# Starting the pass of a linear-attention transformer at another step, with the attention turned ahead of the projections and the query map ahead of the output projection

## The chip, the cores and the metric

The kernel runs on one core of one Trainium2 chip. The metric is the device time of one execution of the whole program in microseconds (us). The engines are named as the profile names them: PE is TensorE's matmuls and PEld its weight loads, DVE is VectorE, ACT is ScalarE, POOL is GpSimd, SP is SyncE, which issues the DMAs.

## What is computed

An input of 8 sequences of 512 tokens with 128 features goes through four stages, each of which adds its result to the input: an attention stage, a mixture of experts, a transformer of six layers with linear attention, and the mixture of experts again. The change touches the transformer stage alone. Cut to that stage:

```python
for l in range(6):                                    # out: 8 sequences x 512 tokens x 128
    q, k, v = out @ Wq[l] + bq[l], out @ Wk[l] + bk[l], out @ Wv[l] + bv[l]   # 16 heads of 8
    Qp, Kp = phi(q, omega[l]), phi(k, omega[l])       # exp(+-x omega - |x|^2 / 2): 16 features
    scores = tril(Qp @ Kp.T)                          # within a chunk of the sequence
    num = scores @ V + Qp @ kv_pre                    # kv_pre: sum over the earlier chunks
    den = scores.sum(-1) + Qp @ ks_pre
    a = (num / (den + eps)) @ Wo[l] + bo[l]
    h1 = layer_norm(out + a) * g1[l] + be1[l]
    y = relu(h1 @ W1[l] + bf1[l]) @ W2[l] + bf2[l]
    out = layer_norm(h1 + y) * g2[l] + be2[l]
```

## The kernel before, in words

`transformer_block` works on one sequence of 512 tokens (four tiles of 128) at a time, all in float32. The work on a sequence in one layer is cut into named steps. Two sequences are under way at once: a *slot* runs the first half of the steps (phase `in`, turn to S0) for one sequence between the steps of the second half (attend, output projection, feed-forward; phases `mix` and `out`) of the sequences before it. There are eight sequences, so eight slots a layer and 48 sequences' worth of work in six layers, with short runs `LEAD`, `FIRST`, `TAIL` and `END` at the two ends of the stage.

What each step is, on which engine:

- `turn`: ACT copies the tokens to `o_now` (L1168), PE transposes them into the PSUM bank w0 (L1022), ACT copies them to `oT` (L1171).
- `project`: PE multiplies by the query weights into w1 and by the key weights into w0 (L1032). ACT evacuates each bank in four activations, the value and the square of each of two halves (L1177, L1179): first `qq` from w1, then `kk` from w0.
- `values`: PE, four token tiles into w1 (L1037); DVE adds the bias into `v_tok` (L1272).
- `mapq`, `mapk`: PE multiplies `qq` into w0 and w1, `kk` into s0 and s1 (L1046); ACT takes the exponential (L1187).
- `keys`, `sums`: transposed keys (L1054, DVE copy L1290) and their sums with the values (L1065, DVE L1295, L1309, L1319).
- `S0`, `S1`: the scores of the two halves of the heads, 64 small matmuls each (L980); DVE masks them into `mixed` (L1328).
- `A0`, `A1`: attend, small matmuls on `mixed` and on the sums into n0 or n1 (L1000, L1004); ACT copies to `num` (L1191).
- `nums`: PE transposes `num` into w0 and n1 (L1089). DVE adds eps to the denominators, takes the reciprocal and multiplies, once for w0 and once for n1 (L1336, L1339, L1341), which makes `att` and frees the two banks.
- `att`: PE transposes `att` into n0 (L1096), ACT copies it to `attT` (L1194).
- `Wo`: PE multiplies `attT` by the output weights into w1 (L1105). DVE adds `o_bias` (L1349; POOL had made it of the tokens and the bias, L939), takes the statistics (L1247, L1251, L1253), waits for POOL's power (L943) and normalises (`Wo_norm`, L1260). POOL scales and shifts (L951, L954).
- `h1`: PE transposes the normalised tile into s2 (L1112), ACT scales it into `oT` (L1197).
- `F1`, `F2`: feed-forward (L1118, then ACT L1202 and DVE L1359; L1126, then DVE L1367, statistics and `F2_norm` as after Wo).
- `weights`: the copies of the next layer's weights for the `in` phase, once a layer. The copies for the `out` phase (`weights_out`: ACT L1155 and L1156, DVE L1237 to L1239, POOL L926 and L927) run once a layer ahead of the first slot, behind a wait for the steps before `slot.steps[0]`.

Each engine runs the steps of its slot in a fixed order: PE, ACT and POOL in the order of `SLOT`, DVE in that of `DVE`. The order within one engine is that of the program, and the engines meet at semaphores alone: `filled` and `emptied` of each PSUM bank, and one for each named event. `wait_free` waits until the bank's last fill has been evacuated, `ready` until the named step's fill has been. So a step placed too early makes everything behind it on its engine wait.

```python
SLOT = ("nums A0 S1 turn project att values Wo mapq A1 mapk h1 keys weights F1 sums S0 F2").split()
DVE = "nums S1 values Wo Wo_norm mapk keys weights F1 sums S0 F2 F2_norm".split()
```

In a layer the first four slots run in an inner loop of two rounds with two slots each, the other four are written out, and an outer loop goes over the first five layers. So each engine jumps back twice a layer, between the last step of one slot and the first of the next (a loop edge, below): F2 and nums on PE, F2 and A0 on ACT, F2_norm and nums on DVE.

Of the kernel before, what the change touches and what calls it, by code (L numbers as in the profile page):

```python
# [214 lines left out]
class AttentionPlan:  # L215
# [5 lines left out]
    LEAD = "X P0 P1 P2 L0 P3 L1 Xn St Yi Ys inc".split()  # L221
# [541 lines left out]
class TransformerPlan:  # L763


    SLOT = ("nums A0 S1 turn project att values Wo mapq A1 mapk h1 keys weights F1 sums S0 F2").split()
    LEAD = "turn project values mapq mapk keys sums S0".split()
    FIRST = "A0 S1 turn project values mapq A1 mapk keys weights sums S0".split()
    TAIL = "nums A0 S1 att Wo A1 h1 F1 F2".split()
    END = "nums att Wo h1 F1 F2".split()  # L770
    DVE = "nums S1 values Wo Wo_norm mapk keys weights F1 sums S0 F2 F2_norm".split()
    WITH = dict(Wo_norm="Wo", F2_norm="F2")
    FILLS = dict(weights="", turn="w0", project="w1 w0", values="w1", mapq="w0 w1", mapk="s0 s1", keys="w0 w1", sums="w0 w1",
                 S0="s0 s1 s2 s3", S1="s0 s1 s2 s3", A0="n0", A1="n1",
# [9 lines left out]
def transformer_block(nc, mem, ins, B):  # L784
# [17 lines left out]
    with ExitStack() as ctx:  # L802
# [3 lines left out]
        def sem(name):  # L806
# [52 lines left out]

        EVENTS = dict(o_now=1, o_bias=1, kz=4, kv_sum=3, v_tok=1, v_pad=1, den=2, inv=2,  # L860
                      stats=8, mv=8, eps=2, rstd=2, xn=8, scaled=2, h1b=1, o_new=1)
        PHASE = {n: "in" if n in ("o_now", "kz", "kv_sum", "v_tok", "v_pad") else "out" for n in EVENTS}
        s = {n: sem(n) for n in EVENTS}
        w_loaded = sem("w_loaded")
        made_in = {n: sem("made_in_" + n) for n in ("act", "dve")}
# [4 lines left out]
        with nc.Block() as block:  # L870
# [44 lines left out]
            @block.gpsimd  # L915
            def _(pool):
                pool.sem_inc(made_out["pool"], 1)

                def weights_in(l, slot):
                    pass  # L920

                def weights_out(l, slot):
                    wait_staged(pool, l, slot)
                    pool.wait_ge(s["o_new"], l * B + (B + 1))
                    pool.nop(nofuse=True)
                    nc.gpsimd.tensor_copy(rows[:].rearrange("p a n -> p (a n)"), next_rows[:, P:7 * P])  # L926
                    nc.gpsimd.tensor_tensor(be1_bf2[:], next_rows[:, 3 * P:4 * P], next_rows[:, 4 * P:5 * P],  # L927
                                            ALU.add).then_inc(made_out["pool"], 1)
                    pool.wait_ge(made_out["pool"], l + 2)
                    pool.nop(nofuse=True)  # L930

                def row(n):
                    return rows[:, n, :].unsqueeze(1).broadcast_to([P, TILES, P])

                def body(step, slot, sequence):
                    if step == "nums":

                        tokens = sequence_of(mem["o"], sequence["out"]).rearrange("p (c d) -> p c d", c=TILES)
                        nc.gpsimd.tensor_tensor(o_bias[:], tokens, row(0), ALU.add).then_inc(s["o_bias"], 1)  # L939
                    elif step in ("Wo", "F2"):  # L940
                        k = ("Wo", "F2").index(step)
                        wait(pool, "eps", slot, k + 1)
                        nc.gpsimd.tensor_tensor(m["rstd"][:], m["var_eps"][:],  # L943
                                                mem["minus_half"][:, 0:TILES], ALU.pow).then_inc(s["rstd"], 1)
                        wait(pool, "xn", slot, TILES * (k + 1))
                        pool.nop(nofuse=True)
                        g, b, out, name = (
                            (row(1), be1_bf2[:].unsqueeze(1).broadcast_to([P, TILES, P]), h1b[:], "h1b"),
                            (row(4), row(5), sequence_of(mem["o"], sequence["out"]).rearrange("p (c d) -> p c d", c=TILES),
                             "o_new"))[k]  # L950
                        nc.gpsimd.tensor_tensor(scaled[:], m["xn"][:], g, ALU.mult).then_inc(s["scaled"], 1)  # L951
                        wait(pool, "scaled", slot, k + 1)
                        pool.nop(nofuse=True)
                        nc.gpsimd.tensor_tensor(out, scaled[:], b, ALU.add).then_inc(s[name], 1)  # L954

                begin(pool, "o_bias rstd scaled h1b o_new")
                pipeline(pool, plan, weights_in, weights_out, body)

            @block.tensor
            def _(pe):  # L960
# [22 lines left out]
                            if u == SPANS - 1:  # L983
                                mm.then_inc(filled[f"s{r}"], 1)

                def attend(slot, t):

                    bank = f"n{t}"
                    if t == 0:
                        pe.wait_ge(s["v_pad"], slot.of("mix") + 2)  # L990
                        pe.wait_ge(s["kv_sum"], slot.of("mix") * 3 + 4)
                    wait_free(pe, bank, slot, f"A{t}")
                    for r in range(4):
                        wait_free(pe, f"s{r}", slot, f"A{t}")
                    pe.nop(nofuse=True)
                    for u in range(SPANS):
                        at = slice(u * SPAN, (u + 1) * SPAN)
                        if u:
                            for r in range(4):
                                nc.tensor.matmul(ps[bank][strip(r), at],  # L1000
                                                 kv[:, u - 1, 8 * t + 2 * r:8 * t + 2 * r + 2, :].rearrange("p h n -> p (h n)"),
                                                 phi_q[slot.parity][t][:, at], start=False, stop=False, skip_group_check=True)
                        for r in range(4):
                            mm = nc.tensor.matmul(ps[bank][strip(r), at],  # L1004
                                                  v_pad[:, u, 4 * t + r, :, :].rearrange("p h n -> p (h n)"),
                                                  mixed[t][r][:, u, :], start=u == 0, stop=u == SPANS - 1,
                                                  skip_group_check=True)
                    mm.then_inc(filled[bank], 1)

                def body(step, slot, sequence):  # L1010
# [64 lines left out]
                            ready(bank, "mapq")  # L1075
                        scores(slot, 0, slot.parity_in)
                    elif step == "S1":
                        pe.wait_ge(s["kz"], slot.of("mix") * 4 + 5)
                        scores(slot, 1, slot.parity)
                    elif step in ("A0", "A1"):  # L1080
                        attend(slot, int(step[1]))
                    elif step == "nums":

                        for t_ in range(2):
# [5 lines left out]
                            t.then_inc(filled[bank], 1)  # L1090
                    elif step == "att":
                        for bank in ("w0", "n1"):
                            ready(bank, "nums")
                        free("n0")
                        for c in range(TILES):
                            t = nc.tensor.transpose(ps["n0"][:, chunk(c)], att[:, c, :], mem["ident"][:])  # L1096
                        t.then_inc(filled["n0"], 1)
                    elif step == "Wo":
                        for made in (made_out["act"], made_out["dve"]):
                            pe.wait_ge(made, slot.layer + 2)  # L1100
                        pe.nop(nofuse=True)
                        ready("n0", "att")
                        free("w1")
                        for c in range(TILES):
                            t = nc.tensor.matmul(ps["w1"][:, chunk(c)], attT[:, chunk(c)], w_o[:],  # L1105
                                                 start=True, stop=True)
                        t.then_inc(filled["w1"], 1)
                    elif step == "h1":
                        wait(pe, "xn", slot, TILES)
                        free("s2")  # L1110
                        for c in range(TILES):
                            t = nc.tensor.transpose(ps["s2"][:, chunk(c)], m["xn"][:, c, :], mem["ident"][:])  # L1112
                        t.then_inc(filled["s2"], 1)
                    elif step == "F1":
                        ready("s2", "h1")
                        for f in range(FT):
                            free(f"s{f}")
                            nc.tensor.matmul(ps[f"s{f}"][:], w_1[:, chunk(f)], h1T[:], start=True,  # L1118
                                             stop=True).then_inc(filled[f"s{f}"], 1)
                    elif step == "F2":  # L1120
                        for f in range(FT):
                            ready(f"s{f}", "F1")
                        free("w1")
                        for c in range(TILES):
                            for f in range(FT):
                                t = nc.tensor.matmul(ps["w1"][:, chunk(c)], hid[f][:, chunk(c)], w_2[:, f, :],  # L1126
                                                     start=f == 0, stop=f == FT - 1)
                        t.then_inc(filled["w1"], 1)
# [698 lines left out]
```

## Time and profile before

| | |
|---|---|
| median of 3 runs | 4180.23 us (4180.0 to 4197.69) |
| the profiled execution | 4184.42 us, its span 4182.6 us |
| granted TensorE clock over the span | 0.939 of full |
| transformer stage | about 1800 us of the span, from some 2000 to some 3800 us |
| busy over the whole span | PE 87%, PEld 66%, DVE 62%, ACT 41%, POOL 22% |

A row of a timeline gives the start, the duration, the engine, the line, the operation and its tiles, merged over successive instructions of a kind (x4 is four of them); in square brackets is the engine's idle time before it and what ended that. A matmul here is of float32 and stands as two instructions in the trace, so a product of 128x512 is x2. The mean of one instruction is its duration and not its share of the stream, as matmuls overlap. A granted clock of 1.00 is TensorE's 2.4 GHz, 0.50 is 1.2 GHz.

### The profile page before, as it was taken

The page shows a single profiled execution, that of the slowest core. Times are in us where ns is not written, and L with a number is a line of the kernel's source. Part 1 is how long each engine was busy: PE and PEld are TensorE (multiplying, and loading weights), DVE is VectorE, ACT ScalarE, POOL GpSimd, SP SyncE. Part 2 cuts the span into 40 slices and gives each one's busy share as a digit, 9 for nine tenths or more (in the row PEclk, how much of TensorE's full clock was granted, in tenths as well). Part 3 has the DMA queues.
Part 4 walks back from the last instruction along what each step waited for, and adds up shares of the span by engine and source line. Part 5 has one row for each costly group of instructions (what it writes and reads, how often), then busy time and mean ns, then how long its engine had stood idle before and what let it go on. Part 6 is the DMA issues. An engine that isn't in the chain of part 4 may idle for free. (4 is left out here: it accounts for less than half of the span.)

```text
span 4182.6 us, 105516 instructions
## 1 busy us (share of the span) xinstructions
PE 3633.0 (87%) x39640; PEld 2780.1 (66%) x39640; DVE 2605.9 (62%) x6838; ACT 1712.6 (41%) x3438; POOL 901.5 (22%) x781
## 2 busy tenths in 40 slices
PE   4999999999999998996788888888888888886998
PEld 3767677777677776885566566666566666664887
DVE  4555555556555556887466666666666666665887
ACT  2555555555555553332333333333333333332332
POOL 3222232322223230000112222222222222221000
PEclk9999999999999999998888999999999889987999
DMA  2000000000000000000000000000000000000000
GB/s 86 24 28 21 28 23 25 26 25 24 27 25 23 24 23 4 1 1 13 14 2 2 15 2 2 15 2 2 15 2 3 15 2 2 2 2 0 1 0 21
DMA packets 38339, 59.63 MB, mean 14 GB/s; under 512 B 6960, under 2 KB 16688, under 8 KB 37552
## 3 DMA queue, kind: packets, MB, share of 16 engines
q1 hardware_dynamic: 37936, 53.78, 3.8%
q8 instruction: 312, 5.11, 0.5%
q14 instruction: 91, 0.75, 0.1%
HBM read 18.10 MB, written 2.10 MB: 5 GB/s over the span
## 5 line engine op out<-in xcount | busy, mean ns | idle before, releaser
L662 ACT ACTIVATE a_prob<-a_s,a_shift,a_scale 128x128 f32<-128x128 f32 (+3 forms) x512 | 312.0, 613 | 486.2 <-DVE a_shift L745 486.1
L943 POOL TENSOR_TENSOR t_rstd<-t_var_eps,minus_half 128x4 f32<-128x4 f32 x96 | 97.6, 1017 | 1219.3 <-DVE t_var_eps L1253 1219.3
L1539 ACT ACTIVATE ffn_silu<-ffn_ps_g 128x512 f32<-128x512 f32 x272 | 161.3, 599 | 382.7 <-PE ffn_ps_g L1489 370.6
L1482 PEld LDWEIGHTS ffn_ps_y<-moe_down,ffn_hidden 128*128 128x128 f32 x2176 | 282.1, 191 | 41.4 <-issue 19.9
L1482 PE MATMUL ffn_ps_y<-moe_down,ffn_hidden 128*128 128x128 f32 x2176 | 288.1, 275 | 17.4 <-DVE ffn_acc L1643 17.4
L1191 ACT COPY t_num<-t_n 128x512 f32<-128x512 f32 x96 | 56.3, 586 | 570.9 <-PE t_n L1004 570.9
L1643 DVE SCALAR_TENSOR_TENSOR ffn_acc<-ffn_ps_y,ffn_combine,ffn_acc 128x128 f32<-128x128 f32 x960 | 269.8, 345 | 8.9 <-DVE ffn_acc L1643 1.8
L1328 DVE TENSOR_TENSOR t_mixed<-t_s,upto 128x512 f32<-128x512 f32 x384 | 238.4, 683 | 21.6 <-PE t_s L980 20.2
L1655 DVE TENSOR_TENSOR ffn_hidden<-ffn_silu,ffn_ps_u 128x512 f32<-128x512 f32 x272 | 185.5, 684 | 106.2 <-ACT ffn_silu L1539 74.6
L742 DVE TENSOR_REDUCE a_neg_max<-a_s 128x2 f32<-128x256 f32 (+3 forms) x256 | 208.8, 816 | 68.1 <-PE a_s L565 65.6
L413 POOL TENSOR_TENSOR a_k_sin<-a_k_swap,sin_swap 128x512 f32<-128x512 f32 x64 | 81.5, 1274 | 733.3 <-DMA a_k_swap<-a_k_own 733.3
L594 PE MATMUL a_z<-a_probT,a_tok 128*64 128x128 f32 x2560 | 179.3, 278 | 40.8 <-ACT a_probT L651 40.8
L696 DVE TENSOR_TENSOR a_lin<-a_a,lin_mask 128x512 f32<-128x512 f32 x256 | 165.0, 687 | 79.0 <-PE a_a L489 79.0
L1004 PE MATMUL t_n<-t_mixed,t_v_pad 128*32 128x64 f32 x6144 | 197.1, 228 | 16.2 <-issue 8.5
L581 PE MATMUL a_t<-ident,a_prob 128*128 128x128 f32 x1280 | 203.2, 283 | 8.1 <-ACT a_prob L662 4.2
L561 PE MATMUL a_s<-a_keys,a_query 64*128 64x128 f32 (+3 forms) x1024 | 203.7, 471 | 1.1 <-issue 0.5
L1004 PEld LDWEIGHTS t_n<-t_mixed,t_v_pad 128*32 128x32 f32 x6144 | 150.6, 115 | 80.1 <-issue 80.0
L980 PE MATMUL t_s<-t_phi_q,t_kz 32*128 32x64 f32 x6144 | 197.2, 274 | 6.0 <-issue 5.4
L980 PEld LDWEIGHTS t_s<-t_phi_q,t_kz 32*128 32x128 f32 x6144 | 184.2, 187 | 16.9 <-issue 8.2
L581 PEld LDWEIGHTS a_t<-ident,a_prob 128*128 128x128 f32 x1280 | 150.3, 144 | 66.8 <-issue 50.6
L651 ACT COPY a_probT<-a_t 128x512 f32<-128x512 f32 (+2 forms) x384 | 188.1, 528 | 5.8 <-PE a_t L581 3.9
L1126 PE MATMUL t_w<-t_w,t_hid 128*128 128x128 f32 x1536 | 184.2, 278 | 2.3 <-DVE t_hid L1359 2.3
(209 smaller groups left out, 8878.8 us busy)
## 6 DMA issues: line engine op xcount, KB each, us to landing
a_k_swap<-a_k_own SPq DMA_DIRECT2D x128, 128.0 KB, 2.1
a_y_swap<-a_y_own SPq DMA_DIRECT2D x128, 128.0 KB, 2.0
a_staged<-in_pairs SPq DMA_DIRECT2D x8, 384.0 KB, 4.0
t_next<-in_t_w SPq DMA_DIRECT2D x12, 256.0 KB, 3.1
t_next_rows<-in_t_rows SPq DMA_DIRECT2D x6, 448.0 KB, 4.1
x<-in_x SPq DMA_DIRECT2D x8, 256.0 KB, 5.3
out<-x SPq DMA_DIRECT2D x1, 2048.0 KB, 8.7
t_next_sq<-in_t_sq SPq DMA_DIRECT2D x6, 256.0 KB, 2.7
```

What stands on the lines that cost most here:

```text
L561: nc.tensor.matmul(ps[f"s{h}"][:, 0:(c + 1) * P], query[slot.parity][rows(h), own], keys[slot.parity][rows(h), 0:(c + 1) * P], start=True, ...
L581: t = nc.tensor.transpose(ps[bank][:, (at + j) * P:(at + j + 1) * P], prob[c % 2][h][:, j * P:(j + 1) * P], mem["ident"][:])
L651: nc.scalar.copy(probT[c % 2][:, hs, 0:n], ps[bank][:, 0:2 * n // len(banks)].rearrange("p (h n) -> p h n", n=n)).then_inc(emptied[bank], 1)
L662: nc.scalar.activation(prob[c % 2][h][:, 0:(c + 1) * P], ps[f"s{h}"][:, 0:(c + 1) * P], ACT.Exp, bias=shift[:, k:k + 1], scale=scale[slot. ...
L742: nc.vector.tensor_reduce(neg_max[:, two], ps_s[:, :, 0:(c + 1) * P], AX.X, ALU.max, negate=True).then_inc(s["negs"], 1)
L980: mm = nc.tensor.matmul(ps[f"s{r}"][:, u * SPAN:(u + 1) * SPAN], kz[t][strip(r), u, :, :].rearrange("p h n -> p (h n)"), phi_q[parity][t][ ...
L1004: mm = nc.tensor.matmul(ps[bank][strip(r), at], v_pad[:, u, 4 * t + r, :, :].rearrange("p h n -> p (h n)"), mixed[t][r][:, u, :], start=u ...
L1126: t = nc.tensor.matmul(ps["w1"][:, chunk(c)], hid[f][:, chunk(c)], w_2[:, f, :], start=f == 0, stop=f == FT - 1)
L1328: nc.vector.tensor_tensor(mixed[t_][r][:], ps[f"s{r}"][:].rearrange("p (u n) -> p u n", u=SPANS), mem["upto"][:].unsqueeze(1).broadcast_to ...
L1482: t = nc.tensor.matmul(ps_y[e % 2][:, c * P:(c + 1) * P], hidden[e % 3][:, c * P:(c + 1) * P], w_down[:, e * P:(e + 1) * P], start=True, s ...
L1643: t = nc.vector.scalar_tensor_tensor(acc[:, c, :], y, combine[parity][:, c, e:e + 1], acc[:, c, :], ALU.mult, ALU.add)
L1655: nc.vector.tensor_tensor(hidden[e % 3][:], silu[e % 2][:], ps_u[e % 2][:], ALU.mult).then_inc(hid_done, 1)
```

## The change

The slot begins at `turn` instead of at `nums`, so that `nums A0 S1` stand at its end. Read as a ring, PE's and ACT's order differs from before in two places: `att` now comes right behind `turn`, ahead of `project`, and `mapq` comes ahead of `Wo`. DVE's `nums` comes ahead of `F2_norm`, where it came behind it. POOL's `o_bias` moves from `nums` to the start of `Wo`, which is the next thing that POOL does after F2's `o_new`, as before. `LEAD` takes over `A0 S1` and `FIRST` takes `nums A0 S1` at its end. What is waited for stays the same, with the counts fitted to the new place of the steps. The loop edges now lie between `S1` and `turn` on PE, between `A0` and `turn` on ACT and between `S1` and `values` on DVE; the copies of `weights_out` lie there too. No operation is added or taken away.

```diff
@@ class TransformerPlan
-    SLOT = ("nums A0 S1 turn project att values Wo mapq A1 mapk h1 keys weights F1 sums S0 F2").split()
-    LEAD = "turn project values mapq mapk keys sums S0".split()
-    FIRST = "A0 S1 turn project values mapq A1 mapk keys weights sums S0".split()
-    TAIL = "nums A0 S1 att Wo A1 h1 F1 F2".split()
-    END = "nums att Wo h1 F1 F2".split()
-    DVE = "nums S1 values Wo Wo_norm mapk keys weights F1 sums S0 F2 F2_norm".split()
+    SLOT = ("turn att project values mapq Wo A1 mapk h1 keys weights F1 sums S0 F2 nums A0 S1").split()
+    LEAD = "turn project values mapq mapk keys sums S0 A0 S1".split()
+    FIRST = "turn project values mapq A1 mapk keys weights sums S0 nums A0 S1".split()
+    TAIL = "att Wo A1 h1 F1 F2 nums".split()
+    END = "att Wo h1 F1 F2".split()
+    DVE = "values Wo Wo_norm mapk keys weights F1 sums S0 F2 nums F2_norm S1".split()
@@ events
-        PHASE = {n: "in" if n in ("o_now", "kz", "kv_sum", "v_tok", "v_pad") else "out" for n in EVENTS}
+        PHASE = {n: "in" if n in ("o_now", "kz", "kv_sum", "v_tok", "v_pad") else "mix" if n in ("den", "inv") else "out"
+                 for n in EVENTS}
@@ gpsimd body
-                    if step == "nums":
+                    if step == "Wo":
                         tokens = sequence_of(mem["o"], sequence["out"]).rearrange("p (c d) -> p c d", c=TILES)
                         nc.gpsimd.tensor_tensor(o_bias[:], tokens, row(0), ALU.add).then_inc(s["o_bias"], 1)
-                    elif step in ("Wo", "F2"):
+                    if step in ("Wo", "F2"):
@@ tensor
-                def attend(slot, t):
+                def attend(slot, t, parity):
...
-                        pe.wait_ge(s["v_pad"], slot.of("mix") + 2)
-                        pe.wait_ge(s["kv_sum"], slot.of("mix") * 3 + 4)
+                        wait(pe, "v_pad", slot, 1)
+                        wait(pe, "kv_sum", slot, 3)
...
                     elif step == "S1":
-                        pe.wait_ge(s["kz"], slot.of("mix") * 4 + 5)
-                        scores(slot, 1, slot.parity)
-                    elif step in ("A0", "A1"):
-                        attend(slot, int(step[1]))
+                        wait(pe, "kz", slot, 4)
+                        scores(slot, 1, slot.parity_in)
+                    elif step == "A0":
+                        attend(slot, 0, slot.parity_in)
+                    elif step == "A1":
+                        attend(slot, 1, slot.parity)
...
                     elif step == "att":
                         for bank in ("w0", "n1"):
-                            ready(bank, "nums")
+                            wait_free(pe, bank, slot, slot.steps[0])
```

## Rows read from the trace of the kernel before

**Rows 1.** The profile's page, its span and its first section (busy time)

```profile
span 4182.6 us, 105516 instructions
PE 3633.0 (87%) x39640; PEld 2780.1 (66%) x39640; DVE 2605.9 (62%) x6838; ACT 1712.6 (41%) x3438; POOL 901.5 (22%) x781
```

**Rows 2.** Stretches of one slot: busy us (instructions) of each engine; granted clock, DMA

```profile
2532.00:2545.00 13.00, 10.18 (x60) 5.68 (x62) 6.34 (x18) 7.53 (x12) 2.71 (x3) 0.74 0.01 1
2549.00:2562.00 13.00, 12.92 (x131) 9.98 (x130) 10.15 (x21) 4.36 (x9) 1.16 (x1) 1.00 0.01 3
```

**Rows 3.** PE's waits in the stage: total us, times, longest

```profile
PE t_w L1105 <- ACT t_attT L1194: 106.0, 48, 2.3
PE t_w L1022 <- DVE t_att L1341: 36.4, 39, 2.0
PE t_w L1032 <- ACT t_oT L1171: 35.1, 47, 0.8
```

**Rows 4.** PE's timeline, a slot of common length: start, duration, instructions, idle before

```profile
2528.91 2.01 PE L980 MATMUL t_s<-t_phi_q,t_kz 32*128 32x64 f32 x64
...
2531.79 0.66 PE L1022 MATMUL t_w<-ident,t_o_now 128*128 128x128 f32 x4 [0.87 <-DVE t_att L1341]
2533.19 3.78 PE L1032 MATMUL t_w<-t_oT,t_w_in 128*128 128x512 f32 x4 [0.75 <-ACT t_oT L1171]
...
2541.61 1.15 PE L1105 MATMUL t_w<-t_w_o,t_attT 128*128 128x128 f32 x8 [1.77 <-ACT t_attT L1194]
...
2547.94 1.98 PE L1046 MATMUL t_s<-t_kk,t_omega 128*128 128x512 f32 x4
2549.76 0.60 PE L1112 MATMUL t_s<-ident,t_xn 128*128 128x128 f32 x4
```

**Rows 5.** ACT's timeline of the same slot

```profile
2535.30 0.68 ACT L1177 ACTIVATE t_qq<-t_w,t_cols_in 64x512 f32<-64x512 f32 x1 [2.24 <-PE t_w L1032]
...
2540.89 0.59 ACT L1194 COPY t_attT<-t_n 128x512 f32<-128x512 f32 x1
...
2549.10 0.60 ACT L1187 ACTIVATE t_phi_k<-t_s 128x512 f32<-128x512 f32 x1 [0.46 <-PE t_s L1046]
2549.96 0.60 ACT L1187 ACTIVATE t_phi_k<-t_s 128x512 f32<-128x512 f32 x1 [0.26 <-PE t_s L1046]
```

**Rows 6.** DVE's timeline of the same slot

```profile
2528.36 0.17 DVE L1253 TENSOR_SCALAR t_var_eps<-t_mean_var 128x4 f32<-128x4 f32 x1
...
2532.25 0.42 DVE L1341 TENSOR_TENSOR t_att<-t_n,t_inv 128x256 f32<-128x256 f32 x1
...
2546.22 1.12 DVE L1260 TENSOR_SCALAR t_xn<-t_o_bias,t_mean_var,t_rstd 128x128 f32<-128x128 f32 x4 [1.13 <-POOL t_rstd L943]
```

**Rows 7.** PE's timeline of the shortest slot, from one S1 to the next

```profile
2756.96 2.01 PE L980 MATMUL t_s<-t_phi_q,t_kz 32*128 32x64 f32 x64
...
2776.22 0.60 PE L1112 MATMUL t_s<-ident,t_xn 128*128 128x128 f32 x4
...
2791.86 2.01 PE L980 MATMUL t_s<-t_phi_q,t_kz 32*128 32x64 f32 x64
```

**Rows 8.** Groups of PE's instructions in the stage: busy us, mean ns of one

```profile
L1126 PE MATMUL t_w<-t_w,t_hid 128*128 128x128 f32 x1504 | 180.4, 278 | 1.0 <-DVE t_hid L1359 1.0
...
L1046 PE MATMUL t_w<-t_qq,t_omega 128*128 128x512 f32 x184 | 137.9, 890 | 0.0
...
L1046 PE MATMUL t_s<-t_kk,t_omega 128*128 128x512 f32 x184 | 91.3, 618 | 0.0
L1105 PE MATMUL t_w<-t_w_o,t_attT 128*128 128x128 f32 x376 | 82.6, 388 | 105.4 <-ACT t_attT L1194 105.4
```

**Rows 9.** The copy of w_2, once a layer: ns min/median/max, first and last start

```profile
L1239 DVE COPY t_w<-t_next x6: 425/1040/1040, 2045.5 to 3534.7; 128x512 f32<-128x512 f32 x6
```

**Rows 10.** PE's and DVE's timelines at one loop edge

```profile
2638.64 0.65 PE L1089 MATMUL t_w<-ident,t_num 128*128 128x128 f32 x4 [2.01 <-issue]
...
2643.48 0.59 DVE L1237 COPY t_cols_v<-t_next_cols 128x6 f32<-128x6 f32 x1 [2.28 <-issue]
```

More of the change, by code:

```diff
@@ L1001, in attend @@
                                                  kv[:, u - 1, 8 * t + 2 * r:8 * t + 2 * r + 2, :].rearrange("p h n -> p (h n)"),
-                                                 phi_q[slot.parity][t][:, at], start=False, stop=False, skip_group_check=True)
+                                                 phi_q[parity][t][:, at], start=False, stop=False, skip_group_check=True)
                         for r in range(4):
```

## The prediction

> **What bounds the kernel now.** I read the page first: PE is busy for 87% of the span and no other engine for more than 62% [rows 1]. That alone would say that reordering can't bring much. The stretches of one slot say otherwise. Over 13 us in the feed-forward half PE is busy for 12.92 us at a granted clock of 1.00; over the 13 us behind S1 it is busy for 10.18 us at a clock of 0.74 [rows 2]. A mean of 0.74 between 1.00 and 0.50 is 52% of the stretch at 1.2 GHz, and a matmul at that level takes longer and so looks busy. So one half of a slot is bound by PE's work, and this change leaves it alone; the other, from the end of S1 to the start of h1, is bound by a chain of waits, and there the steps are moved.
>
> PE's waits name the links: 106.0 us for `attT` ahead of Wo, 36.4 us for DVE's `att` ahead of turn, 35.1 us for `oT` ahead of project [rows 3], 177.5 us or 3.7 us a slot. The timelines say why each is there. DVE makes `att` only after it has normalised F2's result, so w0 is freed late and turn starts 0.87 us after S1's end at 2530.92. Project waits 0.75 us for ACT's copy of `oT`. ACT then evacuates qq and kk in one go from 2535.30 to `attT` at 2540.89, and only behind these comes the copy for which Wo waits [rows 4, 5]. The stretch takes 2549.76 - 2530.92 = 18.84 us in this slot and 2776.22 - 2758.97 = 17.25 us in the shortest [rows 4, 7]. From S1 to S1 the shortest slot takes 34.90 us; the slot of common length takes 1.59 us more, 36.49, all of it in this stretch.
>
> **The new stretch, link by link.** I count from the end of S1 (zero), at full clock, with durations of the common slot.
>
> *Turn.* DVE's `nums` now follows the variance (ends 2528.53) without the wait for POOL and the normalisation. Now the second `att` ends at 2532.67, 1.88 us behind the normalisation's end at 2530.79 (`att` is six operations directly behind it). In the new order it ends at 2528.53 + 1.9, about 2530.4, and the first, which frees w0, 0.95 us earlier [rows 4, 6]. Both lie before S1's end, so turn starts at zero and `att` on PE finds its input ready. What pays is `F2_norm`: 1.9 us of nums less the 1.1 us for which DVE waited for POOL anyway [rows 6], so 0.8 us later, on a tile that isn't read for several slots. S1's masks end no later than before. Nothing on PE waits for either. Gain 0.87 us.
>
> *Project and att.* Project now starts 1.40 us after turn starts [rows 4], so at 1.40 still; but four transposes of `att` (0.6 us) fill PE's wait for `oT`, and ACT copies `attT` at 1.3 to 1.9, when it waited before. So att costs nothing at either place, and its copy of 0.6 us leaves the queue behind kk. In the new stretch PE has had 0.1 us of idleness before project instead of 1.62, so I take project at full clock: its first bank reaches ACT 1.16 us after its start, as `phi_k` (2549.10) follows mapk (2547.94) [rows 4, 5], where in the common slot it took 2.11 (2535.30 - 2533.19). ACT starts qq at 2.56 and is through with kk 5.59 us later [rows 5], at 8.15.
>
> *Mapq* needs w0, which kk frees, so it starts at 8.2; values, at 5.4, fits into the wait as now. That mapq waited behind Wo before and stands ahead of it now is no gain of its own: both need the end of kk. *Wo* needs w1 again, which the second exponential frees: mapk to the end of the second `phi_k` takes 2550.56 - 2547.94 = 2.62 us [rows 4, 5], so Wo starts at 10.8 + 0.1 = 10.9. This is a new wait, of some 0.8 us, and behind it on PE stand A1, mapk and h1.
>
> *h1.* From Wo's start to the end of the normalisation are 2547.34 - 2541.61 = 5.73 us [rows 4, 6], so h1 can start at 16.7. PE itself arrives there at 10.9 + 1.0 + 1.9 (A1) + 1.85 (mapk) = 15.65: what was late by PE's own work is now late by DVE's chain, and 1.0 us of PE's time is idle but covers a slow clock in A1 and mapk. Sum: 16.7 us where the shortest slot has 17.25, so a slot of 34.90 - 0.55 = 34.35 us. DVE's products behind h1 keep their distance to it.
>
> **The clock** is the unknown. Before, TensorE fell to 1.2 GHz in the stretches after turn's and project's waits and again around Wo and mapq. Mapq's matmuls take 890 ns on average where mapk's of the same shape take 618, so 4 x 0.272 = 1.09 us a slot; Wo's take 388 where F2's take 278, 8 x 0.110 = 0.88 us [rows 8]; together 1.97 us. In the new order mapq and Wo are both on the path. The bounds are nothing (full clock) and all of it: at 1.2 GHz mapq and Wo need twice their 1.95 and 1.15 us, 3.1 us more. PE idles there from 3.4 to 8.2 apart from values and again before Wo, so the clock will still fall in some slots. But one idle stretch stands where three stood, so I take less than half of the old loss, 0.85 us. A slot: 35.2 us.
>
> On this the Trainium skill speaks against the change. Its page "TensorE: Matmul & The Clock Gate", section "HAM oscillation — how this bites in real kernels", says that a waiting stretch between bursts of matmuls sends the clock back to half, every time round. The trace agrees that it falls (0.74, rows 2); if it did so in every slot for all of mapq and Wo, the loss would be the upper bound, the third rival.
>
> **The loop edges.** A layer takes (3534.7 - 2045.5) / 5 = 297.84 us [rows 9]; 8 x 36.49 are 291.9, so its two edges cost 5.9 us. At an edge PE stands 2.01 us for nothing that the profile shows, DVE 2.28 us, and at the layer's edge DVE's copies follow before it makes `att` [rows 10]. In the new order DVE's gap and copies fall between S1's masks (end 3.3) and values (its input at 6.6): 3.3 + 2.3 + 1.9 = 7.5, then v_tok until 8.8, which frees w1 in time for mapq's second bank at 9.1. PE's gap stays exposed, now ahead of turn, and the clock behind it will be low for project. 5.5 us a layer.
>
> The page "Runtime: NRT & Kernel Launch", section "Instruction fetch mechanics", says that a taken branch whose target isn't at hand stalls the fetch; that fits the 2.01 us and says that they stay wherever the edge is put.
>
> **Sum.** A layer: 8 x 35.2 + 5.5 = 287.1 us, 10.7 less. The 46 full slots are 5.75 layers' worth: 61.6 us. The short runs at the ends have the same steps; I count them at nothing. Against the profiled execution's 4184.4 us: 4122.8. The median of the runs is 4.2 us lower than it, so 4118.6; I say 4118.
>
> **Rivals.**
> 1. *The clock stays up.* A loss of 0.1 us: 8 x 34.45 + 5.5 = 281.1, 16.7 us less a layer, 96 in all, 4084. For it: att fills the first gap, and a shorter ring changes when the clock falls. Against: 4.8 us with only values in them.
> 2. *The clock falls as before.* The old loss of 1.97 us on mapq and Wo: 8 x 36.3 + 5.5 = 295.9, 11 us less in all, 4169. The freed waits come back as slow matmuls, and the measurement can't tell it from no change.
> 3. *Slower.* Mapq and Wo were in part beside each other's waits; now Wo, and DVE's chain behind it, come last in line behind mapq and ACT's exponential. With both at 1.2 GHz in every slot the loss is 3.1 us: 8 x 37.45 + 5.5 = 305.1, 42 us more, 4222. It decides from a loss of (297.84 - 5.5) / 8 - 34.35 = 2.2 us a slot.
> 4. *ACT's loop edge is uncovered.* ACT's edge lay in its long wait before A0's copy. Now it lies between A0's copy and `o_now`, for which turn waits, and at a layer's edge the copies of `w_o` wait there for S1. A gap like PE's runs beside PE's own and starts earlier, so at least nothing is lost; if ACT ends 1.5 us later than PE at each of 12 edges it is 18 us: 4136.
>
> **Chances and range.** The forecast, with its own range 4100 to 4150, 55%; rival 1, 13%; rival 2, 12%; rival 3, 10%; rival 4, 10%. Leaving rival 3 out, the range is 4084 to 4172. The kernel's measurement can tell about 0.5% (21 us) from no change: faster 0.78, within it 0.12, slower 0.10.
>
> **What would show it.** Right: PE's wait of turn for DVE gone, ACT's `attT` next to `oT`, mapq waiting for `kk`, Wo for `phi_q`, and h1 now waiting for `t_xn` by about 1 us; the distance between copies of w_2 at 287 us a layer. Wrong: mapq's mean near 890 ns or above and Wo's near 430 (rival 2 or 3); a wait of turn for ACT's `o_now` (rival 4); a wait of sums for `k_tok`, which would mean that DVE's masks of the keys, now beside POOL's scaling, have become slower.

## The result and the profile after

The changed kernel takes 4209.9 us (median; 4207.8 to 4214.7) against 4183.3 us before: the ratio is 1.0059, with a 95% interval of 1.0032 to 1.0085. By the ratio it is slower by 25 us, where I had forecast 62 us less (4118 against 4180). The time lies between the rivals 2 (4169) and 3 (4222), nearer to the third.

The page of the changed kernel, to be held against [rows 1], with the granted clock in slices:

```profile
span 4212.9 us, 105523 instructions
PE 3660.5 (87%) x39640; PEld 2803.4 (67%) x39640; DVE 2642.2 (63%) x6838; ACT 1708.6 (41%) x3438; POOL 913.9 (22%) x781
PEclk9999999999999998997899889888888888887999
```

The clock's slices before:

```profile
PEclk9999999999999999998888999999999889987999
```

The same 39640 matmuls keep PE busy for 27.5 us longer. In the transformer stage, from the 20th slice on, most of the clock's slices now read 8, where more than half read 9 before.

PE's timeline of one slot of common length in the changed kernel, from S1 to h1, as [rows 4]:

```profile
2504.73 2.01 PE L981 MATMUL t_s<-t_phi_q,t_kz 32*128 32x64 f32 x64
2506.67 0.66 PE L1023 MATMUL t_w<-ident,t_o_now 128*128 128x128 f32 x4
2507.16 0.60 PE L1099 MATMUL t_n<-ident,t_att 128*128 128x128 f32 x4
2508.08 1.98 PE L1033 MATMUL t_w<-t_oT,t_w_in 128*128 128x512 f32 x4 [0.32 <-ACT t_oT L1174]
2512.06 1.16 PE L1038 MATMUL t_w<-t_w_in,t_oT 128*128 128x128 f32 x8 [2.00 <-ACT t_qq L1182]
2514.85 3.78 PE L1047 MATMUL t_w<-t_qq,t_omega 128*128 128x512 f32 x4 [1.63 <-ACT t_kk L1182]
2519.32 2.07 PE L1108 MATMUL t_w<-t_w_o,t_attT 128*128 128x128 f32 x8 [0.69 <-ACT t_phi_q L1190]
...
2524.48 1.98 PE L1047 MATMUL t_s<-t_kk,t_omega 128*128 128x512 f32 x4
2526.30 0.60 PE L1115 MATMUL t_s<-ident,t_xn 128*128 128x128 f32 x4
```

S1 ends at 2506.74. Counted from there project starts at 1.34 (walk: 1.40), values at 5.32 (5.4) and mapq at 8.11 (8.2): up to here every link came as worked out. Then mapq takes 3.78 us and Wo 2.07, and A1, between Wo and mapk, 3.1 us where I had 1.9. h1 starts at 19.56 instead of 16.7.

The busy times of the engines and the granted clock in this slot, with the columns of [rows 2]: from the end of S1 to the start of h1, then in project, mapq, Wo, most of A1, and mapk:

```profile
2506.80:2526.40 19.60, 14.97 (x157) 9.30 (x158) 7.53 (x23) 8.90 (x14) 5.11 (x5) 0.74 0.01 2
2508.08:2510.06 1.98, 1.98 (x4) 0.67 (x4) 1.61 (x3) 1.17 (x3) 1.76 (x2) 1.00 0.00 0
2514.85:2518.63 3.78, 3.78 (x4) 1.17 (x4) 0.00 (x0) 0.60 (x1) 0.00 (x0) 0.50 0.02 4
2519.32:2521.39 2.07, 2.07 (x12) 1.85 (x16) 0.00 (x0) 0.00 (x0) 0.00 (x0) 0.50 0.00 0
2521.39:2524.10 2.71, 2.71 (x105) 2.71 (x109) 2.12 (x10) 0.00 (x0) 0.31 (x1) 0.50 0.02 6
2524.48:2526.30 1.82, 1.82 (x13) 0.81 (x6) 1.15 (x5) 1.18 (x2) 0.52 (x2) 1.00 0.00 0
```

So project and mapk have the full clock, and mapq, Wo and A1 between them 1.2 GHz throughout. In 41 of the 45 full slots that the trace shows whole, mapq takes 3.4 to 3.8 us; in the other four it takes 1.98.

PE's waits in the stage, against [rows 3], and the groups of mapq and Wo, against [rows 8]:

```profile
PE t_w L1038 <- ACT t_qq L1182: 91.6, 48, 2.0
PE t_w L1047 <- ACT t_kk L1182: 71.5, 48, 1.7
PE t_w L1023 <- issue: 33.3, 10, 3.7
PE t_w L1108 <- ACT t_phi_q L1190: 31.8, 46, 0.8
PE t_s L1115 <- DVE t_xn L1263: 19.8, 13, 6.2
PE t_w L1033 <- ACT t_oT L1174: 11.9, 39, 0.7
```

```profile
L1047 PE MATMUL t_w<-t_qq,t_omega 128*128 128x512 f32 x184 | 164.7, 1047 | 68.8 <-ACT t_kk L1182 68.8
...
L1108 PE MATMUL t_w<-t_w_o,t_attT 128*128 128x128 f32 x376 | 81.0, 382 | 32.5 <-ACT t_phi_q L1190 31.8 <-ACT t_attT L1197 0.7
```

The wait for `att` (36.4 us) is gone, of that for `attT` (106.0 us) 1.4 us are left, and that for `oT` fell from 35.1 to 11.9 us. But the wait of values for `qq` grew (from 40.1 us), those of mapq for `kk` (2.6 us before) and of Wo for `phi_q` are new, and mapq's matmuls went from 890 to 1047 ns. The copy of w_2 gives the length of a layer, as [rows 9]:

```profile
L1242 DVE COPY t_w<-t_next x6: 415/676/1039, 2058.7 to 3561.6; 128x512 f32<-128x512 f32 x6
```

(3561.6 - 2058.7) / 5 = 300.6 us against 297.8.

### The profile page after: what moved, and what is told of

Same layout as the page of the kernel before. It is cut to its first block and busy times, and to the rows that moved or that the text cites. A ratio compares the mean times of both kernels' runs of the same rounds, so it can differ in the third digit from the quotient of the medians.

```text
span 4212.9 us, 105523 instructions
## 1 busy us (share of the span) xinstructions
PE 3660.5 (87%) x39640; PEld 2803.4 (67%) x39640; DVE 2642.2 (63%) x6838; ACT 1708.6 (41%) x3438; POOL 913.9 (22%) x781
## 5 line engine op out<-in xcount | busy, mean ns | idle before, releaser
L1047 PE MATMUL t_w<-t_qq,t_omega 128*128 128x512 f32 x192 | 172.0, 1048 | 71.5 <-ACT t_kk L1182 71.5
L1005 PE MATMUL t_n<-t_mixed,t_v_pad 128*32 128x64 f32 x6144 | 219.1, 244 | 7.2 <-DVE t_mixed L1331 7.1
L1352 DVE TENSOR_TENSOR t_o_bias<-t_w,t_o_bias 128x512 f32<-128x512 f32 x48 | 33.2, 692 | 292.3 <-PE t_w L1108 286.2
L1275 DVE TENSOR_TENSOR t_v_tok<-t_w,t_bv 128x512 f32<-128x512 f32 x96 | 61.5, 682 | 224.1 <-PE t_w L1038 224.1
L1001 PE MATMUL t_n<-t_phi_q,t_kv 128*32 128x64 f32 x5376 | 193.2, 244 | 9.1 <-issue 9.1
```

The lines of the kernel that those rows point to most:

```text
L1001: nc.tensor.matmul(ps[bank][strip(r), at], kv[:, u - 1, 8 * t + 2 * r:8 * t + 2 * r + 2, :].rearrange("p h n -> p (h n)"), phi_q[parity][t ...
L1005: mm = nc.tensor.matmul(ps[bank][strip(r), at], v_pad[:, u, 4 * t + r, :, :].rearrange("p h n -> p (h n)"), mixed[t][r][:, u, :], start=u ...
```

## The experiments

Each was run beside the kernel before, whose median was 4181 to 4187 us from set to set; the ratios are against those runs. Differences between two variants are of their medians, so those between sets are good to some 6 us. Means per slot are of the 45 full slots that a trace shows whole; a slot is "at an edge" when a standstill at a jump back falls into it (12 of the 45, in the old order 13), and "away from the edges" otherwise.

My theory after the result, called *clock* below: PE is idle from project to `kk`'s end but for values, so the clock is at 1.2 GHz when mapq, Wo and A1 come. The rivals: Wo stands behind mapq and its exponential, and DVE's chain with it (*order*); the loop edges cost more at their new place (*edge*).

**1. Which of the moved steps does it?** Three variants of the changed kernel, which differ in the places of att and Wo alone.

e1_rotate:

```diff
-    SLOT = ("turn att project values mapq Wo A1 mapk h1 keys weights F1 sums S0 F2 nums A0 S1").split()
+    SLOT = ("turn project att values Wo mapq A1 mapk h1 keys weights F1 sums S0 F2 nums A0 S1").split()
```

> The changed kernel with att back behind project and Wo back ahead of mapq: what is left of the change is the start of the slot at turn (the loop edges and the copies of the out-phase weights lie there) and DVE's nums ahead of F2_norm. If the loss comes from the new order of att, mapq and Wo (clock or chain), this kernel keeps the 0.87 us a slot ahead of turn and lands at 4145 to 4175. If it comes from the place of the loop edges, it is at or above 4195.

Measured: 4137.5 us, ratio to before 0.9892 (0.9868 to 0.9915). The start at turn and the earlier `nums` alone are worth 47 us, somewhat more than expected. The edges at their new place are not the fault.

e2_att_early:

```diff
+    SLOT = ("turn att project values Wo mapq A1 mapk h1 keys weights F1 sums S0 F2 nums A0 S1").split()
```

> The changed kernel with Wo ahead of mapq again and att still ahead of project. By the theory that Wo's place behind mapq and its exponential is the fault (Wo at 10.9 us behind S1, then DVE's chain), Wo can now start when v_tok frees w1, at about 8.0, and h1 at about 15: 4115 or less. By the theory that the clock is the fault (PE idle from project to kk's end but for values, then everything at 1.2 GHz), Wo, mapq and A1 are still slow, 3 to 4 us on a path of 15: 4165 to 4190.

Measured: 4090.1 us, 0.9779 (0.9755 to 0.9804). That is the order theory's number, 120 us below the changed kernel, for the exchange of two steps. But the exchange touches the clock as well: mapq's mean is 820 ns where the changed kernel has 1047 (Wo's is 391 against 382), so the 120 us are not the order's alone. Part 3 holds the clock up in both orders.

e3_mapq_first:

```diff
+    SLOT = ("turn project att values mapq Wo A1 mapk h1 keys weights F1 sums S0 F2 nums A0 S1").split()
```

> The changed kernel with att back behind project, mapq still ahead of Wo. Wo's place decides: 4205 to 4215 as the changed kernel. If att's place decides (its four transposes fill PE's idle stretch behind project and keep the clock up), 4170 or less, and mapq's mean duration falls well under 1048 ns.

Measured: 4152.2 us, 0.9929 (0.9906 to 0.9952); the changed kernel is 58 us slower. With mapq first Wo waits for `phi_q` and not for `attT`, so att's place should be of no weight to the chain. Its groups of mapq and Wo:

```profile
L1047 PE MATMUL t_w<-t_qq,t_omega 128*128 128x512 f32 x184 | 117.3, 771 | 74.3 <-ACT t_kk L1182 74.3
L1108 PE MATMUL t_w<-t_w_o,t_attT 128*128 128x128 f32 x368 | 61.5, 318 | 31.8 <-ACT t_phi_q L1190 31.8
```

771 ns instead of 1047, with much the same waits ahead (74.3 and 31.8 us). Four transposes, 0.6 us of work, behind project instead of ahead of it made the difference. That speaks for the clock. ACT's order changed along with PE's, but in the common slots of both kernels mapq starts 8.11 us behind S1, so ACT's new order moved nothing ahead of it. The next runs leave ACT's order alone.

**2. Is it the clock?** Matmuls are repeated in the idle stretches. They write the same results again, so no wait becomes shorter; PE has only more to do.

e4_filler (the key projection three times, the values twice):

```diff
                         for bank, n in (("w1", 0), ("w0", 1)):
                             free(bank)
-                            nc.tensor.matmul(ps[bank][:], w_in[:, n, :], oT[:], start=True,
-                                             stop=True).then_inc(filled[bank], 1)
+                            for again in range(3 if n else 1):
+                                t = nc.tensor.matmul(ps[bank][:], w_in[:, n, :], oT[:], start=True, stop=True)
+                            t.then_inc(filled[bank], 1)
                     elif step == "values":
                         free("w1")
-                        for c in range(TILES):
+                        for c in list(range(TILES)) * 2:
```

> The changed kernel with matmuls repeated in the two idle stretches: the key projection three times instead of once, the values twice (same results, written again). Nothing waits for less. If the clock is the fault, mapq and Wo run at 2.4 GHz, mapq's mean falls from 1048 ns towards 620, and the time to 4090 to 4140 in spite of some 2.7 us more work a slot. If the chain through w1 and DVE is the fault, it stays at 4210 or gets slower.

Measured: 4145.4 us, 0.9910 (0.9885 to 0.9934), 64 us faster than the changed kernel with more to do, though 5 us short of the range that I expected. Its timeline of PE in one slot, and the clock from the end of S1 (2460.06) to h1:

```profile
2461.40 3.69 PE L1034 MATMUL t_w<-t_oT,t_w_in 128*128 128x512 f32 x8 [0.32 <-ACT t_oT L1175]
2465.38 2.05 PE L1039 MATMUL t_w<-t_w_in,t_oT 128*128 128x128 f32 x16 [0.28 <-ACT t_qq L1183]
2468.17 1.98 PE L1048 MATMUL t_w<-t_qq,t_omega 128*128 128x512 f32 x4 [0.74 <-ACT t_kk L1183]
2470.84 1.16 PE L1109 MATMUL t_w<-t_w_o,t_attT 128*128 128x128 f32 x8 [0.69 <-ACT t_phi_q L1191]
...
2476.62 0.66 PE L1116 MATMUL t_s<-ident,t_xn 128*128 128x128 f32 x4 [0.90 <-DVE t_xn L1264]
```

```profile
2460.10:2476.60 16.50, 13.60 (x168) 8.08 (x168) 7.00 (x21) 9.51 (x15) 4.47 (x4) 1.00 0.01 2
```

This is the walk of the prediction at full clock: mapq at 8.11 (walk 8.2), Wo at 10.78 (10.9), h1 at 16.56 (16.7), and PE waits 0.90 us for `t_xn` (1.0). Between this slot and that of the changed kernel lie 3.0 us, and the only difference ahead of mapq is PE's work.

Three microseconds in each of 46 slots would be 138 us and not 64. Two things take the rest. The mean from S1 to h1 falls by 1.97 us only (20.03 to 18.06), since the slots at an edge gain nothing: from S1 to S1 they take 39.68 us in the changed kernel and 40.19 here, the others 36.89 and 34.95. And S1 itself grows from 2.03 to 2.70 us on average, for waits that no semaphore explains (18.4 us in 31 times where the changed kernel has 0.6 us in 2). What is left is 1.30 us a slot, 60 us.

e8_key_twice and e11_values_twice (the changed kernel with one of the two repeats, the key projection twice or the values twice):

> The changed kernel with the key projection twice, 0.86 us of matmuls more in the idle stretch behind project and nothing else. att's four transposes moved back there (0.6 us) had brought 58 us. If that came of PE's work in this stretch keeping the clock up, and not of att's own place, this lands at 4135 to 4165. If it came of ACT's or DVE's order, it stays at 4205 to 4215.

> The changed kernel with values twice (1.0 us of matmuls more, between values and mapq), the key projection once. If any work between project and mapq keeps the clock up, as the key projection twice did (4131), it lands at 4130 to 4160. If it is the stretch between project and values that counts, it stays at 4190 to 4215.

Measured: 4131.3 us, 0.9873 (0.9846 to 0.9899), and 4143.8 us, 0.9898 (0.9877 to 0.9920). Mapq's mean is 721 and 668 ns. The first is 4 us below its expected range, the second within. With ACT's and DVE's order untouched, 0.86 us of matmuls more a slot took 79 us off, in whichever of the two stretches it is 66 us at least. So it is PE's idleness that costs, by way of the clock, and work in either stretch will do.

e5_before_filler (the kernel before, with the repeats of e4):

> The kernel before with the same repeated matmuls (key projection three times, values twice). By the walk at full clock its h1 starts 16.5 us behind S1 (turn at 0.9, project 2.3, kk's end 9.0, attT 9.6, Wo 9.75, mapq 10.7, A1 12.6, h1 16.4) where it has 18.4 now: 1.9 us a slot, 87 us, so about 4095. Then the cold clock was half of what bound the kernel before too. If the clock matters only in the changed order, it stays at 4175 to 4190.

Measured: 4160.6 us, 0.9937 (0.9914 to 0.9961). The direction is the clock theory's; the size is a quarter of the 87 us that I expected. Mapq and Wo are at full clock there (619 and 287 ns), and the stretch that I had walked came out as said: from S1 to h1 it takes 16.63 us on average instead of 18.51, 1.88 us less where I had 1.9. It is the other half of the slot that took back 0.82 us, and 0.64 of these are S1, which grew from 2.18 to 2.82 us. PE's waits in S1, first before and then in e5:

```profile
PE t_s L980 <- issue: 5.4, 9, 0.8
```

```profile
PE t_s L980 <- issue: 20.2, 37, 1.3
```

PE stands still in the midst of S1 for nothing that the profile shows. That leaves 1.06 us a slot or 49 us, and the profiled execution is in fact 43 us faster than the one before. The median of the seven executions lies 19 us above it (they go from 4141 to 4169 us), and why they differ so I can't tell.

**3. What is the order worth when the clock is up?** e6_att_proj2 is e2 with the key projection three times, e12_key_thrice the changed kernel with the same; they differ in whether Wo or mapq comes first.

> att early, Wo ahead of mapq (4090) with the key projection three times. If the clock falls for the idle stretch behind project, this takes most of the cold matmuls away: h1 at 15 to 15.5 instead of 16.9, 4010 to 4040. If only the stretch between values and Wo matters, it stays within 10 us of 4090.

> The changed kernel with the key projection three times: it differs from the version at 4043 in nothing but mapq standing ahead of Wo. By the walk at full clock h1 is at 16.7 us with mapq first and at 14.8 with Wo first: 1.9 us a slot, 85 us, so 4120 to 4135. If the order of the two is of no weight once the clock is up, it is 4043 too.

Measured: e6 4043.0 us, 0.9667 (0.9643 to 0.9691); e12 4136.3 us, 0.9881 (0.9857 to 0.9904). The order is worth 93 us, 2.0 us in each of 46 slots, where the walk says 1.9. Both are 1 to 3 us above the ranges that I expected. The timeline of e6, where S1 ends at 2460.30:

```profile
2461.73 3.69 PE L1034 MATMUL t_w<-t_oT,t_w_in 128*128 128x512 f32 x8 [0.32 <-ACT t_oT L1175]
2465.70 1.16 PE L1039 MATMUL t_w<-t_w_in,t_oT 128*128 128x128 f32 x8 [0.28 <-ACT t_qq L1183]
2468.24 1.16 PE L1109 MATMUL t_w<-t_w_o,t_attT 128*128 128x128 f32 x8 [1.37 <-DVE t_v_tok L1276]
2469.23 2.07 PE L1048 MATMUL t_w<-t_qq,t_omega 128*128 128x512 f32 x4
2473.05 1.98 PE L1048 MATMUL t_s<-t_kk,t_omega 128*128 128x512 f32 x4
2474.87 0.60 PE L1116 MATMUL t_s<-ident,t_xn 128*128 128x128 f32 x4
```

Since `attT` is ready at 2, Wo waits only for w1, which `v_tok` frees, and runs at 7.9 in the time for which mapq has to wait for `kk` anyway. DVE's chain starts 2.8 us earlier, `phi_q` is no longer ahead of it, and PE arrives at h1 without a stop.

e7_att_both (e6 and two more products of 128x512 into the free bank s3 ahead of Wo):

> As the one before, with two more products of 128x512 into the free bank s3 between values and Wo, so that PE has no long idle stretch left. Full clock nearly throughout, h1 at 14.8: 3995 to 4015. If these matmuls delay Wo instead, it is slower than the one before.

Measured: 4046.4 us, 0.9667 (0.9648 to 0.9687), as e6. That is 31 us above the range that I expected. Mapq's mean fell from 656 to 619 ns, and away from the edges the stretch from S1 to h1 became 0.3 us shorter (14.86 to 14.56), but S1 itself grew by as much (2.36 to 2.64), so from S1 to S1 nothing is gained (32.81 and 32.83).

**4. The other terms.** e10_nums_late is e6 with DVE's nums behind F2_norm again:

```diff
-    DVE = "values Wo Wo_norm mapk keys weights F1 sums S0 F2 nums F2_norm S1".split()
+    DVE = "values Wo Wo_norm mapk keys weights F1 sums S0 F2 F2_norm nums S1".split()
```

> The same version (4043) with DVE's nums behind F2_norm again, as before the change. By the walk the first att frees w0 0.9 us behind S1 and the second is done at 1.8, for which PE's att, now ahead of project, waits: project at 2.45 instead of 1.35, 1.1 us a slot, 50 us: 4085 to 4100. If DVE's order is of no weight, 4043.

Measured: 4088.7 us, 0.9769 (0.9751 to 0.9787), 46 us above e6. DVE's order was worth what the walk says. PE's waits for it come back:

```profile
PE t_w L1023 <- DVE t_att L1345: 18.6, 32, 1.1
...
PE t_n L1100 <- DVE t_att L1345: 8.1, 28, 0.3
```

e9_unrolled4 is e6 with `UNROLLED = 4`:

> The version with att early, Wo ahead of mapq and the key projection three times (4043), with the first four slots of a layer written out as one round of the inner loop instead of two rounds of two. The slot at each jump back is 37 to 38 us there against 32 to 33.7 for the others. If the jump itself is what costs, 4.5 us a layer go: 4010 to 4022. If it is the place in the layer or the entry and exit of the loop, nothing changes.

Measured: 4014.7 us, 0.9599 (0.9577 to 0.9621), 28 us below e6 and the fastest version of all. PE's wait ahead of turn, first of e6 and then of e9:

```profile
PE t_w L1023 <- issue: 36.6, 12, 3.8
```

```profile
PE t_w L1023 <- issue: 16.0, 4, 4.2
```

20.6 us of PE's standstill at turn are gone with the jump in the middle of the layer. The layer is (3390.7 - 2054.7) / 5 = 267.2 us long by the copy of w_2, against (3410.5 - 2053.0) / 5 = 271.5 in e6.

## Why the prediction was wrong

**What bounds the kernel** was right: the stretch from S1 to h1, and there the chain. Every run that moved a step there changed the time.

**Turn** was right. e1, with little else left of the change, gains 47 us (1.0 us a slot, 0.87 expected); e10 loses 46 when it is undone.

**Project and att** was right as to project (1.34 us behind S1, at full clock), and wrong in the sentence that att costs nothing at either place. On the chain it costs nothing (mapq starts at 8.11 with att at either place). But behind project its transposes were work in an idle stretch, and with mapq first their removal cost 58 us (e3 against the changed kernel). With Wo first the same move gains 47 us (e1 to e2), for there Wo does wait for `attT`.

**Mapq and Wo** was right in its times (e4: 8.1, 10.8 and h1 at 16.6) and missed a comparison: I held the new stretch against the old one alone, 16.7 against 17.25, and so the two moves counted as one small gain. Each for itself, they are a large gain (att early) and a larger loss (Wo behind mapq): 2.0 us a slot at full clock (e6 against e12), and 120 us as the change has it, with the clock's share in it (e2 against the changed kernel).

**The clock** is the term that failed. I took a loss of 0.85 us a slot, less than half of the old 1.97, since one idle stretch stood where three had stood. The layer of 300.6 us gives (300.6 - 5.5) / 8 - 34.35 = 2.54 us, and the 33 slots away from the edges the same: 36.89 - 34.35. The 1.69 us too few are 13.5 us a layer and 78 of the 92 us by which the forecast missed. Of the rest, 5 us lie ahead of the stage, whose first turn starts at 1992.5 us in the changed kernel's trace and at 1987.6 in the old one's; the remainder I have not traced.

What told in these runs was not the number of idle stretches but how little PE had to do in them. Behind project it has 1.16 us of work in the 4.8 us up to mapq, and then it pays at mapq in 41 of 45 slots and behind it in 35, where Wo and A1 together take 4.0 to 5.3 us instead of 2.90; the old order had att and values there. Work put back into these stretches, with nothing else touched, brings mapq from 1047 to 721 ns (e8), 668 (e11) and 618 (e4). The loss also took A1, which I held to be covered by DVE's slack: at 1.2 GHz PE itself arrives at h1 after `t_xn`, so h1 waited for `t_xn` 13 times, not 46.

The rule of the Trainium skill that I cited against the change (TensorE: Matmul & The Clock Gate, HAM oscillation — how this bites in real kernels) described this: a stretch of waiting in every round, and a cold burst behind it in every round. The trace agrees, although here the wait was broken up by values into 2.00 and 1.63 us. The third rival had its place, a point of decision (2.2 us) that the measured 2.54 us passes, and an upper price of 3.1. I gave it one chance in ten because my estimate of the loss came from the old order's mean and not from what the new order leaves PE to do.

**The loop edges** cost the 5.5 us a layer that I had said, 300.6 - 8 x 36.89, but that was luck. At full clock they cost about twice as much: in e4, where the copies of w_2 run from 2057.9 to 3510.1 us, the layer is 290.4 us and the edges are 290.4 - 8 x 34.95 = 10.8 us, and in e12 they are 10.2. When the other slots got faster, the slots at an edge did not; why, these runs don't show. For the old order the same count gives 297.8 - 8 x 36.12 = 8.8 us where I had 5.9, since I had taken one slot of 36.49 us for all. So rival 1 with its 4084 lacked some 5 us a layer for the edges, about 30 us in all, and the versions that hold the clock up by repeats pay for them in S1 besides. None with mapq ahead of Wo came below 4131.

PE's standstill ahead of turn, 33.3 us in 10 times, stayed exposed, as said. I have no run that puts a number on rival 4. `t_o_now` ended PE's wait at turn only twice (3.5 us).

## What to carry to other kernels

When steps are moved on an engine whose clock follows its work, add up for the new order what that engine has to do in each waiting stretch, and price the work behind an emptied stretch at half clock first; work with slack is worth most in such a stretch. Price each move for itself and in both orders of its neighbour: here two moves of opposite sign hid in one sum that looked like a small gain. If a stretch must stay empty, repeating a matmul whose result doesn't change is a cheap test of the clock, and here even a gain: 79 us for 0.86 us of work a slot. Then look at the rest of the loop too, since the added work can cost time elsewhere, as S1 shows.

## What I had not expected of the hardware

Repeated matmuls brought standstills of PE in the midst of S1 that no semaphore explains, and S1 became longer with their number in a slot. Its mean is 2.03 us in the changed kernel, 2.18 with 2 matmul instructions more (e8), 2.36 and 2.39 with 4 (e6 and e12), 2.64 and 2.74 with 8 (e7 and e11) and 2.70 with 12 (e4), no more than with 8. PE's waits there are 0.6 us in 2 times in the changed kernel, 5.6 us in 18 in e6, 10.0 us in 30 in e7, 16.7 us in 36 in e11 and 18.4 us in 31 in e4. It matters little which products are repeated: e7 repeats no values. The cause is open.

A jump back at which PE stood still cost 28 us of the whole time for six jumps (e9 against e6), of which 20.6 us are PE's own standstill at turn.
